# A mixture-of-experts layer with causal attention: query loads in shorter pieces, three banks and added products for the first-pass blocks, and GpSimd for the marks' product

## What is computed

```
xn  = layernorm(x)                             # x: 8 x 256 x 256, float32
q, k, v = split(xn @ Wqkv.T + b)               # 16 query heads of 16, one key and one value head
att = softmax(causal(q @ k.T / 4)) @ v         # per batch element and head
a   = att @ out_w.T + out_b
p   = softmax(xn @ w_router.T)                 # 16 experts, 2048 tokens
top 4 experts per token, weights divided by their sum
f   = sum over the 4 of  w * ((silu(xn @ gate_e) * (xn @ up_e)) @ down_e)
out = x + a + f
```

## Time and profile before

| | us |
|---|---|
| median of 3 runs | 453.85 (450.96 to 454.04) |
| the profiled execution | 451.22 |
| its span | 449.3 |
| PE busy | 398.7 (89%) |
| POOL busy | 299.8 (67%) |
| DVE busy | 209.0 (47%) |
| ACT busy | 187.0 (42%) |

### The profile page before, as it was taken

How to read it: one execution, slowest core, us unless ns; L and a number is a source line. 1 busy time by engine, 2 the same in 40 slices (tenths; PEclk the granted TensorE clock), 3 DMA queues, 4 the chain that set the end, 5 groups by cost and what they waited for, 6 DMA issues and landing times.

```text
span 449.3 us, 6428 instructions
## 1 busy us (share of the span) xinstructions
PE 398.7 (89%) x1687; PEld 226.8 (50%) x1688; DVE 209.0 (47%) x514; ACT 187.0 (42%) x439; POOL 299.8 (67%) x323
## 2 busy tenths in 40 slices
PE   3998699799999998999999999999999999898810
PEld 1443245455455544566666666666656666444400
DVE  5878899798887741322322332232233223222200
ACT  4585036467676675333333333333333333233200
POOL 7989111059993571088888888888888888887530
PEclk9999659999999999999999999999999999999965
DMA  7399999989776798045445544544434544544136
GB/s 228 122 214 227 204 206 213 178 167 221 168 174 188 247 288 297 27 69 87 71 78 79 84 69 70 84 79 86 74 66 79 83 76 85 75 75 58 16 59 128
DMA packets 54186, 57.27 MB, mean 127 GB/s; under 512 B 11456, under 2 KB 49008, under 8 KB 53904
## 3 DMA queue, kind: packets, MB, share of 16 engines
q0 software_dynamic: 15440, 21.51, 28.2%
q1 hardware_dynamic: 25760, 22.83, 22.3%
q10 hardware_dynamic: 12960, 12.62, 10.8%
HBM read 37.40 MB, written 23.33 MB: 135 GB/s over the span
## 4 chain that ended last, share of the span: by engine, by line
PE 51%; DVE 13%; issue 11%; POOL 8%; DMA 7%; ACT 3%; SPq 2%; POOLq 0%; DVEq 0%
PE bank L843 19%; PE bank L859 10%; DVE pmax L1202 6%; PE bank L651 5%; PE bank L720 5%; PE bank L709 3%; POOL ks L573 3%; PE bank L833 2%; PE bank L851 2%; PE bank L748 2%; POOL out_dram L587 2%; DMA ks<-xn_d,get_row 2%; DMA odd_d<-late,slots 1%; POOL odd_d L587 1%; DMA out_dram<-late,slots 1%
## 5 line engine op out<-in xcount | busy, mean ns | idle before, releaser
L843 PE MATMUL bank<-wgu,late 128*128 x316 | 149.0, 594 | 1.1 <-ACT late L1076 1.1
L587 POOL DMA_INDIRECT out_dram<-late,slots x40 | 63.1, 1577 | 32.4 <-ACT late L1083 21.3
L859 PE MATMUL bank<-wdn,late 128*128 x316 | 81.5, 380 | 1.4 <-DVE late L1423 1.4
L1072 ACT ACTIVATE late<-bank 128x256 f32<-128x256 f32 x79 | 30.4, 384 | 122.9 <-PE bank L843 122.9
L996 ACT ACTIVATE pt<-bank 128x512 f32<-128x512 f32 x96 | 56.2, 599 | 50.5 <-PE bank L709 49.3
L843 PEld LDWEIGHTS bank<-wgu,late 128*128 128x128 f32 x316 | 53.9, 190 | 39.6 <-issue 39.6
L587 POOL DMA_INDIRECT odd_d<-late,slots x39 | 61.4, 1575 | 15.7 <-issue 8.9
L1202 DVE TRANSPOSE_TENSOR_REDUCE pmax<-bank 128x16 f32<-128x512 f32 x96 | 66.0, 703 | 12.8 <-PE bank L651 12.1
L859 PEld LDWEIGHTS bank<-wdn,late 128*128 128x128 f32 x316 | 53.9, 190 | 6.4 <-issue 2.4
L1416 DVE SCALAR_TENSOR_TENSOR late<-late,ks,bank 128x256 f32<-128x256 f32 x39 | 18.7, 481 | 71.0 <-ACT late L1072 71.0
L573 POOL DMA_INDIRECT ks<-xn_d,get_row x39 | 42.7, 1094 | 12.0 <-issue 8.8
(11 more groups left out here) (152 smaller groups left out, 496.1 us busy)
## 6 DMA issues: line engine op xcount, KB each, us to landing
qs_late<-q_d SPq DMA_DIRECT2D x40, 128.0 KB, 5.4
q_d<-early SPq DMA_DIRECT2D x16, 256.0 KB, 6.5
wgu<-in_L_ffn_w_gate_dram ACTq DMA_DIRECT2D x8, 512.0 KB, 4.7
wgu<-in_L_ffn_w_up_dram ACTq DMA_DIRECT2D x8, 512.0 KB, 6.6
wdn<-in_L_ffn_w_down_dram ACTq DMA_DIRECT2D x8, 512.0 KB, 6.1
qs_wgu<-q_d SPq DMA_DIRECT2D x24, 128.0 KB, 6.1
xs<-in_L_attn_x_dram SPq DMA_DIRECT2D x4, 512.0 KB, 3.9
xn_d<-early SPq DMA_DIRECT2D x4, 512.0 KB, 4.2
```

The source lines that it names most:

```text
L587: pool.indirect_dma_start(odd_d if j % 2 else out_rows, bass.IndirectOffsetOnAxis(ap=slots[:, j:j + 1], axis=0), ys[:, j % YRING, :], None ...
L843: mm = pe.matmul(bank[:, 2 + buf, :], xT[:, buf, c, :], wgu[:, bass.ds(e * KC + c, 1), :], start=(c == 0), stop=(c == KC - 1))
L859: mm = pe.matmul(bank[:, 4 + buf, 0:D], hT[:, buf, c, :], wdn[:, bass.ds(e * FC + c, 1), :], start=(c == 0), stop=(c == FC - 1))
```

## The change

There are six edits.

1. `load_q` issues eight transfers of 64 KB in place of four of 128 KB, and each takes the heads one by one, so its contiguous pieces are 512 bytes instead of 4096.
2. `zero_odd(0)` moves to right behind the first two stores of `xn`, at some 17 us, and `zero_odd(1)` from element 4 to element 3. The store of the choice weights (L421) moves from element 1 to element 4.
3. The second half of the queries of element 2 is loaded after the last stores of projections, behind a wait for the first maxima (`nm_ready`).
4. The first 20 first-pass blocks go through three banks, 0 to 2, instead of two. Bank 2 is the projections' bank, so block 2 waits until the last keys and values have been taken from it.
5. From block 6 of element 0 to block 7 of element 1 PE issues a product of the identity with itself behind each first-pass block (`stay_busy`), 14 in all, whose result nobody reads.
6. `choice_slots` goes. POOL makes the product of marks and slots, in four instructions between `copy_k(3)` and `copy_k(4)`, and `add_slots` waits for it.

```diff
+        def max_bank(N):
+            return N % 3 if N < MAX_AHEAD else N % 2
+
+        def max_bank_free(N):
+            for at in range(N - 1, -1, -1):
+                if max_bank(at) == max_bank(N):
+                    return at + 1
+            return 0
...
             def load_q(b, half):
                 for r in range(4):
-                    sp.dma_start(qs[b % 3][16 * r:16 * r + 16, half].rearrange("p (m h) t -> p m (h t)", m=KC).bitcast(F32),
-                                 q_d[2 * b + half, r % 2].rearrange("m (d h) t -> d m (h t)", d=HD)
-                                 ).then_inc(q_in[b % 3][half], 16)
+                    for m in range(KC):
+                        sp.dma_start(qs[b % 3][16 * r:16 * r + 16, half, m * H // KC:(m + 1) * H // KC].bitcast(F32),
+                                     q_d[2 * b + half, r % 2, m].rearrange("(d h) t -> d h t", d=HD),
+                                     max_dma_last_dim=512).then_inc(q_in[b % 3][half], 16)
...
             store_xn(0)
             store_xn(1)
+            zero_odd(0)
...
-                    for half in range(2):
+                    for half in range(2 if g < 2 else 1):
                         load_q(g, half)
...
+            sp.wait_ge(nm_ready, 1)
+            load_q(2, 1)
             load_k(2 * GW, T)
...
-            zero_odd(0)
...
-                if b == 1:
+                if b == 4:
                     sp.wait_ge(coef_ready, 2)
                     sp.dma_start(xn_d[:, D:D + E].rearrange("(t p) e -> p t e", p=P), logits[:]).then_inc(coef_stored, 16)
-                if b == 4:
+                if b == 3:
                     zero_odd(1)
...
             copy_k(3)
+            pool.wait_ge(k_ready, 8)
+            pool.wait_ge(slots_known, 1)
+            pool.wait_ge(xn_stored[1], 32)
+            for at in range(0, NT, NT // 4):
+                ts = slice(at, at + NT // 4)
+                pool.tensor_tensor(cells[:, ts], onehot[:, ts],
+                                   probs[:, ts].unsqueeze(2).to_broadcast([P, NT // 4, TOP_K, E]), ALU.mult
+                                   ).then_inc(cells_ready, 1)
+            pool.wait_ge(cells_ready, 4)
             copy_k(4)
...
-                if N >= 2:
-                    pe.wait_ge(max_done, N - 1)
+                if max_bank_free(N):
+                    pe.wait_ge(max_done, max_bank_free(N))
+                if N == 2:
+                    pe.wait_ge(vr_ready, NG)
+                    pe.wait_ge(kl_ready, NG)
                 k, q = queries(b, n, 96)
-                pe.matmul(bank[:, N % 2, :], k, q, start=True, stop=True).then_inc(p1_ps, 1)
+                pe.matmul(bank[:, max_bank(N), :], k, q, start=True, stop=True).then_inc(p1_ps, 1)
...
+            def stay_busy():
+                pe.matmul(bank[:, 4, 0:P], ident[:, :], ident[:, :], start=True, stop=True)
+
             for n in range(NB // 3, NB):
                 scores_for_max(0, n)
+                if n == NB // 2:
+                    pe.wait_ge(ql_ready, KC * NG)
+                if n >= NB // 2:
+                    stay_busy()
             for n in range(MAX_AHEAD - NB):
                 scores_for_max(1, n)
+                stay_busy()
...
             def add_slots(part):
+                dve.wait_ge(cells_ready, 2 * part + 2)
```

31 lines of the change are left out of this document (12 added, 19 removed).

## The result

The changed kernel takes 460.6 us (median of 4 runs, 457.67 to 463.19), the one before 452.65 (4 runs): 1.018 times as long, 95% interval 1.014 to 1.022. I had forecast 449.6 us and a range up to 455.5. It is slower, and outside the range.

What follows compares the result with a forecast made beforehand. PE (experts, 300 to 400 us) and POOL (96 to 138 us) bound fixed stretches, so time up to `route_ready` counts. 2.2 + 0 + 0 + 0 + 0.7 = 2.9 us off: 448.3 or 450.95, forecast 449.6, range 443.5 to 455.5.

Steps and rivals of the forecast that it cites:

- the query loads: On SP: doubled issues, 3.4 us instead of 1.7 per half, hidden by 3.9 us of transfer; 0, up to 1.7 lost.
- Rival 3: Elements 1 to 4: doubled issues make queries late, each waits up to 2 us more; 459 us, chance 0.15.
- The moves: First zeros at 17 us, half of element 2's queries behind the last stores: 0 each, 1 us the latter's bad end.
- Three banks: First pass: maxima of blocks 12 to 19 at 0.67 us each; 2.6 us together, 2.2 reaching element 0.
- what counts is when it starts: POOL's comparisons from 96 to 138 us keep their length; the change is worth what it takes off up to `route_ready`.
- Added products: First pass to element 1: 0.2 us each at full clock, 0.4 at half; cost 0, gain taken as 0.
- Rival 1: Element 1: queries come sooner, waits before blocks 36 and 40 go; 7.4 us off, 446.4 us, chance 0.27.
- Rival 2: Elements 0 and 1: clock falls around 60 us instead, low for some 20 us; no gain, 454 us, chance 0.13.
- The marks' product: Moved from DVE into POOL's gap before `copy_k(4)`: cost 0 there, `route_ready` 0.7 us earlier.

Runs made afterwards that it cites:

- two more of the same instructions: The changed kernel with only the second zeros back in element 4 (1.021), and with twelve experts' weight loads issued after the attention (479.0 us).
- the best version: The changed kernel with the old query loads and the second zeros back in element 4: 448.35 us, ratio 0.990 to before.
- all three runs with late weights: Twelve experts' weight loads issued behind the attention, on the changed kernel, on it with old loads and second zeros back, and on before: 479.0, 474.8, 476.9 us.

## Why the prediction was wrong

**The step that failed** is the one on the query loads: "That is just under 3.9, so the transfer hides the issue", and "What stands behind a load on SP (key and query stores, keys, maxima) was behind its data in the same rings already. I take 0". It looked at the transfer only. An issue keeps SP as well, and what stands behind is late for its issue and not for its data. The key store was issued at 35.4 instead of 31.9 us, and ScalarE waited for it 3.5 us in the changed trace, 1.5 and 2.1 in two more of the same instructions; DVE and PE stand in line behind that. The last half of element 2's queries came 3.3 and 2.7 us late in those two. SP, idle for 6.1 us between 59 and 67.6 us before, had no gap above 0.5 us up to 70. Alone, the new loads cost 2.1% and the doubled issues with long pieces 1.6%, that is 7 to 10 us, where I had 0 with 1.7 as the bad end for a load that is waited for. I had worked out this very number (3.4 against 1.7 us per half), and multiplied it by nothing.

**Rival 3** had mechanism and size nearly right: doubled issues, 459 us against 460.6 measured, with a chance of 0.15. Its place was wrong in the main, so the size is partly luck: two thirds of the cost come from the loads of elements 0 to 2, which it did not speak of, and one third from the late ones, where it expected all. My reason against it, that POOL bounds the stretch from 96 us, did not hold: PE's wait of 2.95 us at 135.36 went to the end in full.

**An edit I did not price.** "The moves" dealt with the first zeros and with half of element 2's queries. The second zeros, 1 MB that now go ahead of a query load in element 3, had no term. With the old loads they cost 1% (1.000 against 0.990). In the changed kernel itself nothing that can be told comes back when they are moved (1.021 against 1.018); the wait in element 4 is then there without them.

**Three banks.** The term was right where it was read: 56.1 us for the second pass against 56.2 forecast, maxima at 0.67 us. That it comes through to the end one for one ("what counts is when it starts") holds only with the moves beside it: on before alone the ratio is 1.001, in the best version the bank makes some 1.2%. A likely reason, argued and not shown for this stretch, stood in the rows ahead of time: a DMA share of 0.88 to 1.07 from 40 to 70 us, and slices of 8 and 9 in the earlier trace rows up to 112 us. I read them as traffic beside the bound, not as a bound.

**Added products.** The durations were too low, 0.39 and 0.63 us measured against 0.2 and 0.4; the cost of 0 was right all the same, since DVE sets the step there, the reason given. They keep the clock up, and it brings nothing.

**Rival 1** did not come about: from 29 to 34 us the queries came at 124 GB/s, against 152 before. Whether short pieces could move faster alone isn't shown: at 0.47 us an issue of 64 KB the issues themselves allow no more than some 140 GB/s, an estimate from these two. With as many issues, short and long pieces both came at 134 GB/s in that stretch. **Rival 2** (the clock falls later) is seen in part, 0.57 from 64 to 76 us, but the run without the products takes the same time, so it decides nothing.

**The marks' product.** Hidden on POOL as forecast; its 0.7 us on DVE was not measured alone, and the run without banks (1.001) leaves no room for much. The comparisons' first cast, which follows `route_ready`, stands at 97.05 us instead of 95.73, where I had forecast 92.8.

What stays open: why a single wait of 2 to 3 us comes in just one element, and in which; behind 75 us it was absent in all three runs with late weights, the rest is not shown. Open too are the rate of a load by its rows, and why ScalarE stands still in element 6 in some profiles and not in others.

## What to carry to other kernels

Price every issue twice: once for its own transfer, and once for what stands behind it in the issuing engine's queue, down to the store that someone waits for; a doubled load is free only if nothing behind it is tight and the issuing queue has idle time to give. Where the DMA share is 0.9 or more, as it was here, count the DMA engines as a bound too: time won on PE and DVE came back as waits for data, until transfers left the stretch. Undo the parts one at a time: this change held a version 1% faster than before (all but the pieces and the second zeros), hidden under one that is 1.8% slower.

## What the runs showed of the hardware

- A transfer whose outermost dimension has the size 2 took 12.1% of 16 DMA engines, the time of two: 41 GB/s from 29 to 34 us, where the same queries in transfers of 16 rows came at 152.
- One issue of these query loads keeps SP for 0.43 us in the median, whether it carries 128 KB (0.424) or 64 KB (0.431 in the changed kernel), so halving a transfer doubled the price per byte.
- The same kernel has a stall of 3.2 us on ScalarE in one profile and none in another, and its median moved between 452.2 and 456.3 us from group to group, higher where the profiles have the stall.
- Behind PE's waits of 3.73 and 2.95 us the granted clock was 0.50 from 44 to 46 us and 0.62 from 136 to 140 us in the changed kernel. The interval with the wait of 2.95 us was 3.9 us longer than before's.
